# Self-attention with weighted values of float16 parts, queries and keys placed in three steps, and the work of all heads put in one repeating order

## The chip, the core and the metric

The program runs on one core of one Trainium2 chip. The metric is the device time of one execution, in microseconds (us). The core's engines run beside each other and wait for each other by semaphores only: TensorE (PE) multiplies, VectorE (DVE), ScalarE (ACT) and GpSimd (POOL) do the elementwise work, and SyncE (SP) starts DMA transfers. Each engine takes its instructions strictly in the order in which the program has them, so an instruction that waits holds up all that stand behind it.

## The reference

The kernel computes one layer over x of shape 8 x 512 x 256 in float32: self-attention, attention to a second input, and a block with eight experts. The change touches the first part alone:

```python
x = x + _L0_attn_ref(_layernorm(x, axis=-1), w_q, w_k, w_v, w_o)

q = jnp.einsum('ntc,hdc->nhtd', x, w_q)      # 16 heads of 64
k = jnp.einsum('ntc,hdc->nhtd', x, w_k)
v = jnp.einsum('ntc,hdc->nhtd', x, w_v)
a = jnp.einsum('nhtd,nhsd->nhts', q, k) / jnp.sqrt(dk)
a = jnp.where(mask, -jnp.inf, a)             # causal: keys after the query are masked
a = jax.nn.softmax(a, axis=-1)
y = jnp.einsum('nhts,nhsd->nthd', a, v)
return y.reshape(n, t, -1) @ w_o
```

## The kernel before

`self_attention` works in 32 units: 8 batches times 4 groups of 4 heads. A product of two float32 matrices is made of float16 parts (`split_terms`): each operand is a high part and the low part that rounding left over, and three matmuls (high-high, low-high, high-low) replace one. The steps of a unit are these, with the names that the rest of the text uses.

- Projections (`project_qk`, four calls; `project_v`, two). Each is 12 or 6 matmuls into a PSUM bank `pp`; ACT rounds the result to its high part (`a_nat_q`, `a_nat_k`), DVE writes the low part (`qk_low`, two instructions of 64 partitions each, straight to `QB` and `KA`). Values stay float32 in `V`.
- Placing. SP copies the high parts by eight DMAs of 128 KB to `QA`, `KA`, `KB` (`copy_qk`). A scores matmul then has the high and the low part of one side stacked on the 128 partitions.
- Maxima (`scores_for_max`, 16 per unit). A matmul of 128 queries by the keys up to them goes to a bank `pm`, and DVE takes the row maxima (`reduce_max`, an instruction and a short read of its accumulator). They are turned on PE, negated by ACT (`NMT`) and placed by two small DMAs in a row of `QB` (`place_max`), so that the scores come out of PE with the maximum taken off.
- Scores, exponentials, weighted values (`scores`, `exponentials`, `weighted_values`), 12 slots per unit, three per head: 128 keys by 512 queries, 128 by 384, and 128 by 256 with 128 by 128. Scores go to one of two banks `pS`, ACT writes the exponentials to one of four float32 buffers `PR`, and PE multiplies them with `V` in float32 into a bank `pa`. One half of each `V` tile is ones, so half of `pa` holds the row sums.
- Normalizing and the output projection: `reciprocals` (ACT: Ln, then Exp of its negative), `scale_values` (DVE), `split_values` (POOL), and once per batch `project_out`, 96 matmuls in one piece, and `residual`.

The order is written out by hand. Turn s of the loop holds the front of unit s (projections, placing, maxima) and the back of unit s-1 (scores to normalizing). Slot i of the turn issues the scores of slot i, then in slots 0, 1, 3 and 4 a projection, from slot 5 to 10 the 16 maxima, two or three at a time, and the weighted values of slot i-1. `project_out` of the previous batch stands whole in slot 6 of every fourth turn.

## Time and profile before

| | |
|---|---|
| time, median of 3 runs | 2320.03 us (2316.13 to 2321.22) |
| the profiled execution | 2315.4 us, its span 2313.7 us |
| PE busy over the span | 1958.2 us (85%) |
| DVE, ACT, POOL busy | 1397.7, 1194.2, 699.9 us |
| granted TensorE clock, mean | 0.934 of full speed |

The program has three parts, one after the other. Self-attention fills the first 1010 us. A row of the profile names the source line, the engine, the operation, what is written and what is read (`a_` are the tensors of self-attention), the shape, the count, busy time and the mean duration of one, and then how long the engine stood idle before such rows and for whom. Matmuls overlap: a row's duration is longer than the distance from one matmul's start to the next one's, and that distance is what a matmul costs in a full stream. In a timeline row the first number is the start, the second the duration, and the bracket at the end, where there is one, is the idle time before it with what ended it.

### The profile page before, as it was taken

To read this page: it belongs to the slowest core of one execution; us is meant where nothing else is said; L and a number is where in the kernel's file an instruction comes from. 1 tells how busy PE (TensorE), PEld (TensorE's weight loads), DVE (VectorE), ACT (ScalarE), POOL (GpSimd) and SP (SyncE) were. 2 spreads that over 40 slices of the span, in tenths; PEclk is the share of its full clock that TensorE was granted. 3 is DMA by queue.
4 is the path that set the end of the run, shared out by engine and by line. 5 is a ranking of instruction groups with operands and counts; after the bars stand their busy time and mean duration, and the time that the engine had idled before them with its cause. 6 is when DMAs were issued, how large, how long until landed. Compare 5 with 4: busy or idle time off the path is not lost. (4 is left out here: it accounts for less than half of the span.)

```text
span 2313.7 us, 37956 instructions
## 1 busy us (share of the span) xinstructions
PE 1958.2 (85%) x13464; PEld 1002.0 (43%) x13464; DVE 1397.7 (60%) x3126; ACT 1194.2 (52%) x2157; POOL 699.9 (30%) x693
## 2 busy tenths in 40 slices
PE   4899999999999999967999999847888887459973
PEld 2556565655565656542333233212333333236642
DVE  5665656564656565526878777735677876513344
ACT  2554545454545454534777777743555664125541
POOL 2111101110111111122333333124466666412266
PEclk8999999999999999987999899977999998779996
DMA  5111111111111021123223222200011201133355
GB/s 155 46 40 34 38 37 37 37 38 38 37 32 43 20 46 29 37 63 57 56 56 56 37 50 55 32 18 28 1 37 38 65 28 37 39 101 104 105 161 155
DMA packets 97082, 122.82 MB, mean 53 GB/s; under 512 B 14305, under 2 KB 73985, under 8 KB 96897
## 3 DMA queue, kind: packets, MB, share of 16 engines
q1 hardware_dynamic: 79872, 93.11, 17.1%
q0 software_dynamic: 6144, 16.79, 2.3%
q10 hardware_dynamic: 10880, 10.49, 1.4%
q8 instruction: 112, 1.84, 0.3%
q14 instruction: 74, 0.60, 0.1%
HBM read 52.64 MB, written 33.82 MB: 37 GB/s over the span
## 5 line engine op out<-in xcount | busy, mean ns | idle before, releaser
L1037 DVE TENSOR_REDUCE x_NM<-x_pm 128x1 f32<-128x512 f32 x512 | 342.6, 687 | 108.4 <-PE x_pm L780 106.3
L962 ACT ACTIVATE x_PR<-x_pS 128x512 f32<-128x512 f32 x512 | 300.9, 601 | 115.6 <-PE x_pS L796 108.9
L309 PE MATMUL a_pa<-a_PR,a_V 128*128 128x512 f32 (+3 forms) x1024 | 340.7, 440 | 0.7 <-ACT a_PR L389 0.3
L389 ACT ACTIVATE a_PR<-a_pS 128x384 f32<-128x384 f32 (+1 forms) x384 | 201.4, 525 | 206.7 <-PE a_pS L298 204.3
L471 DVE CUSTOM_DVE_ANT_0 a_pm<-a_pm,a_causal 128x128 f32<-128x128 f32 (+3 forms) x512 | 247.2, 509 | 84.9 <-PE a_pm L284 70.1
L544 POOL CAST a_YT_hi<-a_Y 128x512 f16<-128x512 f32 x64 | 40.2, 628 | 759.1 <-DVE a_Y L479 759.1
L780 PE MATMUL x_pm<-x_KT,x_QT 48*128 48x512 f16 x512 | 198.6, 406 | 22.7 <-DMA x_QT<-q_k_parts 22.0
L796 PE MATMUL x_pS<-x_QT,x_KT 49*128 49x512 f16 x512 | 194.2, 396 | 17.3 <-ACT x_PR L962 16.1
L479 DVE TENSOR_TENSOR a_Y<-a_pa,a_RS 64x512 f32<-64x512 f32 x128 | 88.0, 688 | 181.0 <-ACT a_RS L397 179.8
L309 PEld LDWEIGHTS a_pa<-a_PR,a_V 128*128 128x128 f32 x1024 | 174.7, 192 | 29.8 <-ACT a_PR L389 11.3
L284 PE MATMUL a_pm<-a_KA,a_QA 128*128 128x128 f16 (+3 forms) x512 | 142.5, 308 | 44.9 <-DVE a_NM L471 27.9
L808 PE MATMUL x_pa<-x_PR,x_V 128*32 128x256 f32 x2048 | 168.2, 401 | 1.7
L296 PE MATMUL a_pS<-a_QA,a_KA 128*128 128x512 f16 (+3 forms) x512 | 153.2, 299 | 1.7 <-DMA a_QB<-a_NMT 1.7
L395 ACT ACTIVATE a_RS<-a_pa 64x512 f32<-64x512 f32 x128 | 75.7, 592 | 144.1 <-PE a_pa L309 141.9
L297 PE MATMUL a_pS<-a_QB,a_KB 128*128 128x512 f16 (+3 forms) x512 | 146.5, 299 | 0.0
L796 PEld LDWEIGHTS x_pS<-x_QT,x_KT 49*128 49x128 f16 x512 | 46.7, 93 | 187.2 <-issue 89.4
L2279 PE MATMUL e_pH<-m_w_hi,e_xt 128*128 x320 | 109.7, 385 | 15.7 <-ACT e_xt L2327 6.6
L258 PE MATMUL a_pp<-a_xT_hi,a_wqk_hi 128*128 128x512 f16 x256 | 98.8, 386 | 23.2 <-DVE a_QB L461 15.8
L1774 ACT ACTIVATE f_PR<-f_pS 128x512 f32<-128x512 f32 x128 | 69.4, 594 | 83.3 <-PE f_pS L1624 83.3
L461 DVE SCALAR_TENSOR_TENSOR a_KA<-a_pp,a_nat_k 64x512 f16<-64x512 f32 x128 | 88.2, 689 | 36.1 <-ACT a_nat_k L377 35.2
L2369 DVE SCALAR_TENSOR_TENSOR e_TH<-e_TH,e_pH 128x512 f32<-128x512 f32 x40 | 27.5, 687 | 134.8 <-ACT e_TH L2333 134.8
L298 PE MATMUL a_pS<-mask_kq,idb 128*128 128x128 bf16 x512 | 105.5, 219 | 0.0
(360 smaller groups left out, 4519.4 us busy)
## 6 DMA issues: line engine op xcount, KB each, us to landing
a_QA<-a_nat_q SPq DMA_DIRECT2D x128, 128.0 KB, 2.3
e_xr<-sent SPq DMA_DIRECT2D x80, 128.0 KB
made<-e_eo ACTq DMA_DIRECT2D x40, 256.0 KB
a_KA<-a_nat_k SPq DMA_DIRECT2D x64, 128.0 KB, 2.3
a_KB<-a_nat_k SPq DMA_DIRECT2D x64, 128.0 KB, 2.4
x_KT<-q_k_parts SPq DMA_DIRECT2D x48, 128.0 KB, 4.3
x_QT<-q_k_parts SPq DMA_DIRECT2D x48, 128.0 KB, 4.4
f_w_stage<-in_w SPq DMA_DIRECT2D x12, 512.0 KB
```

The costliest lines, as they stand in the source:

```text
L284: eng.matmul(o, QA[:, par, side, pair, t * P:(t + 1) * P], KA[:, par, side, pair, 0:(t + 1) * P], start=True, stop=True).then_inc(s_mx, 1)
L296: eng.matmul(o, KA[:, par, side, pair, ks], QA[:, par, side, pair, qs], start=True, stop=False)
L297: eng.matmul(o, KB[:, par, side, pair, ks], QB[:, par, side, pair, qs], start=False, stop=False)
L309: m = eng.matmul(pa[j % 2][:, P * kc:T], V[:, u % 2, kc, j, :], PR[:, i % 4, at:at + T - P * kc], start=(kc == 0), stop=(kc == TT - 1))
L389: eng.activation(PR[:, i % 4, 0:n], pS[i % 2][:, 0:n], ACT.Exp, scale=SCALE).then_inc(s_e, 1)
L471: eng.tensor_tensor_reduce(out=pm[i % 2][:, 0:n], in0=pm[i % 2][:, 0:n], in1=causal[:, T - n:T], scale=1.0, scalar=NEG, op0=ALU.add, op1=A ...
L780: eng.matmul(ring_bank("max", v, n)[:, :], QT[r, par, pair, t * P:(t + 1) * P], KT[r, par, pair, :], start=True, stop=True).then_inc(s_mx, 1)
L796: eng.matmul(pS[i % 2][:, :], KT[r, par, pair, kc * P:(kc + 1) * P], QT[r, par, pair, :], start=True, stop=True).then_inc(s_s, 1)
L808: m = eng.matmul(pa[2 * D * j:2 * D * (j + 1), q], V[:, b % 2, kc, GH * g + j, :], PR[:, kc, j, q], start=(kc == 0 and half == 0), stop=(k ...
L962: eng.activation(PR[:, kc, j, :], pS[i % 2][:, :], ACT.Exp, scale=SCALE).then_inc(s_e, 1)
L1037: eng.tensor_reduce(NM[:, v % 2, c:c + 1], ring_bank("max", v, n)[:, :], AX.X, ALU.max, negate=True).then_inc(s_red, 1)
L2279: m = eng.matmul(pH[p % 2][:, h, :], xt[:, p % 2, h, x, kc, :], w13[ww][:, kc, bass.ds(e, 1), :].rearrange("p a f -> p (a f)"), start=(i = ...
```

## The change

The loop of turns is gone. Each engine has its steps as threads (for PE: weighted values, scores, maxima, projections), each step has a place in time from the table `PLACE`, repeated every `TURN`, and `side_by_side` merges the threads by these numbers. The numbers are sort keys only; nothing waits for a time. Beside the order, the steps themselves change:

- The exponential is computed twice from the same bank: once in float32 (`PR`, now three buffers) and once rounded to float16 (`P_hi`, four buffers). POOL subtracts them to the low part (`P_lo`). PE multiplies with three float16 matmuls per former float32 one. `V` has a high part from ACT and a low part from DVE. `LIFT` raises the exponentials by a constant factor that normalizing takes out again.
- A bank `pS` is free when the second exponential has read it (`s_eh`); weighted values wait for the low part (`s_el`).
- Low parts of queries and keys are written by one DVE instruction of 128 partitions to `nat[1]`, and DMAs place them as well: six for queries (`CQ`), four for keys (`CK`), two for the keys' second copy (`CKB`). `QA` and `QB` have three buffers.
- The output projection is cut to one tile of 128 rows per unit, 24 matmuls, five units later; `YT` has two buffers. The second half of the reciprocals is one instruction for two heads.
- The weights are staged in two buffers instead of four.

```diff
+def side_by_side(*threads):
+    at = [next(t, None) for t in threads]
+    while any(a is not None for a in at):
+        n = min((a, i) for i, a in enumerate(at) if a is not None)[1]
+        at[n] = next(threads[n], None)
...
-    weights = Weights(names, chunks, 4, 4 * C)
+    weights = Weights(names, chunks, 2, 4 * C)
...
-    QA, QB, KA, KB = (sb(n, [P, 2, 2, 2, T], F16) for n in ("QA", "QB", "KA", "KB"))
+    RQ = 3
+    QA, QB = (sb(n, [P, RQ, 2, 2, T], F16) for n in ("QA", "QB"))
+    KA, KB = (sb(n, [P, 2, 2, 2, T], F16) for n in ("KA", "KB"))
...
-    PR = sb("PR", [P, 4, T], F32)
+    RF, RH = 3, 4
+    PR = sb("PR", [P, RF, T], F32)
+    P16 = [sb(f"P_{n}", [P, RH, T], F16) for n in ("hi", "lo")]
...
+    TURN = 27.0
+    PLACE = {
+        ("PE", "QK"): (0, 0.988, 14.218, 17.436),
...
+        ("SP", "CK"): (21.044,),
...
+    }
...
+    def at(engine, step, u, i=0):
+        return u * TURN + PLACE[engine, step][i]
...
-            if i == 0:
-                eng.wait_ge(s_cp[par], CPS * (u // 2 + 1))
-                eng.wait_ge(s_lo, 4 * u + 4)
-                after(eng, s_ne, u)
...
-            after(eng, s_e, US * u + i - 1)
...
-        def weighted_values(u, i):
-            j, sl = i // NS, i % NS
-            eng.wait_ge(s_e, US * u + i + 1)
-            if sl == 0:
-                after(eng, s_y, GH * u + j - 1)
-            if i == 0:
-                eng.wait_ge(s_vout, 2 * u + 2)
-            for kc, at in SLOTS[sl]:
-                m = eng.matmul(pa[j % 2][:, P * kc:T], V[:, u % 2, kc, j, :], PR[:, i % 4, at:at + T - P * kc],
-                               start=(kc == 0), stop=(kc == TT - 1))
-            m.then_inc(s_av, 1)
+        def project_out(u):
+            b, t = (u - 5) // NG, (u - 5) % NG
+            for half in range(2):
+                yield at("PE", "WO", u, half)
+                if half == 0:
+                    if u == 5:
+                        eng.wait_ge(weights.split_done, NW)
+                    eng.wait_ge(s_yh, 2 * NG * (b + 1))
+                    eng.wait_ge(s_yl, 2 * NG * (b + 1))
+                    eng.wait_ge(s_vlo, min(2 * u + 1, 2 * NU))
+                    after(eng, s_xr, u - 5)
+                n = 12 * half
+                for pr in range(4 * half, 4 * half + 4):
+                    for w, y in split_terms(*(z[:, pr, :] for z in wo), *(z[:, b % 2, pr, t * P:(t + 1) * P] for z in YT)):
+                        m = eng.matmul(pp[0][:, 0:C], y, w, start=(n == 0), stop=(n == 23))
+                        n += 1
+            m.then_inc(s_wo, 1)
...
+                if i == 0:
+                    eng.wait_ge(s_cq[par], NCQ * (u // 2 + 1))
+                    eng.wait_ge(s_ck[par], NCK * (u // 2 + 1))
...
+                if i == 0:
+                    eng.wait_ge(s_ckb[par], NCKB * (u // 2 + 1))
+                    eng.wait_ge(s_nd[par], 32 * (u // 2 + 1))
+                after(eng, s_eh, US * u + i - 1)
...
+        def weighted_values(u):
+            for i in range(US):
+                yield at("PE", "AV", u, i)
+                j, sl = i // NS, i % NS
+                eng.wait_ge(s_el, US * u + i + 1)
+                if sl == 0:
+                    after(eng, s_y, GH * u + j - 1)
+                if i == 0:
+                    eng.wait_ge(s_vlo, 2 * u + 2)
+                for kc, a in SLOTS[sl]:
+                    for n, (v, p) in enumerate(((0, 0), (1, 0), (0, 1))):
+                        m = eng.matmul(pa[j % 2][:, P * kc:T], V[v][:, u % 2, kc, j, :], P16[p][:, i % RH, a:a + T - P * kc],
+                                       start=(kc == 0 and n == 0), stop=(kc == TT - 1 and n == 2))
+                m.then_inc(s_av, 1)
...
+        side_by_side(over(weighted_values), over(scores), over(scores_for_max), over(projections, NU + 5))
...
-        def exponentials(u, i):
-            n = slot_width(i % NS)
-            eng.wait_ge(s_s, US * u + i + 1)
-            after(eng, s_av, US * u + i - 3)
-            eng.activation(PR[:, i % 4, 0:n], pS[i % 2][:, 0:n], ACT.Exp, scale=SCALE).then_inc(s_e, 1)
+        def exponentials(u):
+            for i in range(US):
+                yield at("ACT", "E", u, i)
+                m, n = US * u + i, slot_width(i % NS)
+                eng.wait_ge(s_s, m + 1)
+                after(eng, s_el, m + 1 - RF)
+                eng.activation(PR[:, m % RF, 0:n], pS[i % 2][:, 0:n], ACT.Exp, scale=SCALE).then_inc(s_e, 1)
+                yield at("ACT", "H", u, i)
+                after(eng, s_av, m + 1 - RH)
+                eng.activation(P16[0][:, m % RH, 0:n], pS[i % 2][:, 0:n], ACT.Exp, scale=SCALE).then_inc(s_eh, 1)
...
-            for side in range(2):
-                rows = slice(side * D, (side + 1) * D)
-                dst, at = (QB, side) if qk == 0 else (KA, 1 - side)
-                i = eng.scalar_tensor_tensor(out=dst[at * D:(at + 1) * D, u % 2, side, pair, :], in0=pp[c % 2][rows, :],
-                                             scalar=1 / WS, in1=nat[qk][rows, pair, :], op0=ALU.mult, op1=ALU.subtract)
...
+                eng.scalar_tensor_tensor(out=nat[1][qk][:, pair, :], in0=pp[c % 2][:, :], scalar=1 / WS,
+                                         in1=nat[0][qk][:, pair, :], op0=ALU.mult, op1=ALU.subtract).then_inc(s_lo, 1)
...
+        def exp_low(u):
+            for i in range(US):
+                yield at("POOL", "LO", u, i)
+                m, n = US * u + i, slot_width(i % NS)
+                eng.wait_ge(s_e, m + 1)
+                eng.wait_ge(s_eh, m + 1)
+                after(eng, s_av, m + 1 - RH)
+                eng.tensor_tensor(P16[1][:, m % RH, 0:n], PR[:, m % RF, 0:n], P16[0][:, m % RH, 0:n],
+                                  ALU.subtract).then_inc(s_el, 1)
...
+        def copies(u):
             par = u % 2
+            yield at("SP", "CQ", u)
+            if u == 0:
+                eng.wait_ge(s_pre, NPRE)
+            eng.wait_ge(s_hi, 4 * u + 2)
+            eng.wait_ge(s_lo, 4 * u + 2)
+            after(eng, s_s, US * (u - RQ + 1))
+            for side, own in enumerate(sides):
+                for rows in sides:
+                    eng.dma_start(QA[rows, u % RQ, side, :, :], nat[0][0][own, :, :]).then_inc(s_cq[par], 16)
+                eng.dma_start(QB[own, u % RQ, side, :, :], nat[1][0][own, :, :]).then_inc(s_cq[par], 16)
+            yield at("SP", "CK", u)
             eng.wait_ge(s_hi, 4 * u + 4)
+            eng.wait_ge(s_lo, 4 * u + 4)
             after(eng, s_s, US * (u - 1))
+            for side, own in enumerate(sides):
+                eng.dma_start(KA[own, par, side, :, :], nat[0][1][own, :, :]).then_inc(s_ck[par], 16)
+                eng.dma_start(KA[sides[1 - side], par, side, :, :], nat[1][1][own, :, :]).then_inc(s_ck[par], 16)
+            yield at("SP", "CKB", u)
+            for side, own in enumerate(sides):
+                eng.dma_start(KB[own, par, side, :, :], nat[0][1][own, :, :]).then_inc(s_ckb[par], 16)
+            yield at("SP", "NP", u)
             eng.wait_ge(s_ne, u + 1)
...
```

How the engines' orders stand, first PE in the middle of a turn. L296 and L448 are scores, L284 and L429 maxima, L309 and L464 weighted values. Before:

```order
L309 MATMUL a_pa<-a_PR,a_V 128x256 [waits a_exp]
L309 MATMUL a_pa<-a_PR,a_V 128x128
L296 MATMUL a_pS<-a_QA,a_KA 128x384 [waits a_exp]
L297 MATMUL a_pS<-a_QB,a_KB 128x384
L298 MATMUL a_pS<-mask_kq,idb 128x128
L284 MATMUL a_pm<-a_KA,a_QA 128x384 [waits a_red]
L284 MATMUL a_pm<-a_KA,a_QA 128x512 [waits a_red]
L309 MATMUL a_pa<-a_PR,a_V 128x512 [waits a_y,a_exp]
```

After:

```order
L429 MATMUL a_pm<-a_KA,a_QA 128x128 [waits a_red]
L464 MATMUL a_pa<-a_P_hi,a_V_hi 128x512 [waits a_y,a_exp_lo]
L464 MATMUL a_pa<-a_P_hi,a_V_lo 128x512
L464 MATMUL a_pa<-a_P_lo,a_V_hi 128x512
L448 MATMUL a_pS<-a_QA,a_KA 128x384 [waits a_exp_hi]
L449 MATMUL a_pS<-a_QB,a_KB 128x384
L450 MATMUL a_pS<-mask_kq,idb 128x128
L429 MATMUL a_pm<-a_KA,a_QA 128x256 [waits a_red]
L429 MATMUL a_pm<-a_KA,a_QA 128x384 [waits a_red]
L464 MATMUL a_pa<-a_P_hi,a_V_hi 128x384 [waits a_exp_lo]
L464 MATMUL a_pa<-a_P_hi,a_V_lo 128x384
L464 MATMUL a_pa<-a_P_lo,a_V_hi 128x384
```

A weighted-values matmul has become three, and it waits for the low part of the exponentials from POOL instead of the exponentials from ACT. The weighted values stand some slots behind their scores, where they stood one slot behind.

ACT in a turn: L389, L509 and L512 are exponentials, L395/L397 and L522/L525 the reciprocals, L377 and L489 high parts, L421 the maxima's copy. Before:

```order
L389 ACTIVATE a_PR<-a_pS 128x384 [waits a_av,a_scores] x2
L389 ACTIVATE a_PR<-a_pS 128x512 [waits a_av,a_scores]
L395 ACTIVATE a_RS<-a_pa 64x512 [waits a_y,a_av]
L397 ACTIVATE a_RS<-a_RS 64x512 [waits a_ln]
L389 ACTIVATE a_PR<-a_pS 128x384 [waits a_av,a_scores] x2
L421 ACTIVATE a_NMT<-a_pm 16x128 [waits a_nm_placed1,a_nm_turned]
L395 ACTIVATE a_RS<-a_pa 64x512 [waits a_y,a_av]
L397 ACTIVATE a_RS<-a_RS 64x512 [waits a_ln]
```

After:

```order
L509 ACTIVATE a_PR<-a_pS 128x384 [waits a_exp_lo,a_scores]
L489 ACTIVATE a_nat_q_hi<-a_pp 128x512 [waits a_q_placed0,a_qk]
L512 ACTIVATE a_P_hi<-a_pS 128x384 [waits a_av]
L489 ACTIVATE a_nat_q_hi<-a_pp 128x512 [waits a_qk]
L509 ACTIVATE a_PR<-a_pS 128x384 [waits a_exp_lo,a_scores]
L512 ACTIVATE a_P_hi<-a_pS 128x384 [waits a_av]
L522 ACTIVATE a_RS<-a_pa 64x512 [waits a_y,a_av]
L509 ACTIVATE a_PR<-a_pS 128x512 [waits a_exp_lo,a_scores]
L512 ACTIVATE a_P_hi<-a_pS 128x512 [waits a_av]
L509 ACTIVATE a_PR<-a_pS 128x384 [waits a_exp_lo,a_scores]
L512 ACTIVATE a_P_hi<-a_pS 128x384 [waits a_av]
L522 ACTIVATE a_RS<-a_pa 64x512 [waits a_y,a_av]
```

Each slot now has two exponentials, the second waiting for a free `P_hi` buffer, and the high parts of the next unit's queries stand between them.

PE where the maxima of a unit begin; the first of them waits for the placed queries and keys. Before:

```order
L296 MATMUL a_pS<-a_QA,a_KA 128x128
L297 MATMUL a_pS<-a_QB,a_KB 128x128
L298 MATMUL a_pS<-mask_kq,idb 128x128
L284 MATMUL a_pm<-a_KA,a_QA 128x128 [waits a_nm_out,a_red,a_lo,a_copied0]
L284 MATMUL a_pm<-a_KA,a_QA 128x256 [waits a_red]
L309 MATMUL a_pa<-a_PR,a_V 128x384 [waits a_exp]
L284 MATMUL a_pm<-a_KA,a_QA 128x384 [waits a_red]
L296 MATMUL a_pS<-a_QA,a_KA 128x512 [waits a_exp]
L297 MATMUL a_pS<-a_QB,a_KB 128x512
L298 MATMUL a_pS<-mask_kq,idb 128x128
```

After:

```order
L448 MATMUL a_pS<-a_QA,a_KA 128x256 [waits a_exp_hi]
L449 MATMUL a_pS<-a_QB,a_KB 128x256
L450 MATMUL a_pS<-mask_kq,idb 128x128
L448 MATMUL a_pS<-a_QA,a_KA 128x128
L449 MATMUL a_pS<-a_QB,a_KB 128x128
L450 MATMUL a_pS<-mask_kq,idb 128x128
L429 MATMUL a_pm<-a_KA,a_QA 128x128 [waits a_nm_out,a_red,a_k_placed1,a_q_placed1]
L429 MATMUL a_pm<-a_KA,a_QA 128x256 [waits a_red]
L448 MATMUL a_pS<-a_QA,a_KA 128x512 [waits a_exp_hi]
L449 MATMUL a_pS<-a_QB,a_KB 128x512
L450 MATMUL a_pS<-mask_kq,idb 128x128
L429 MATMUL a_pm<-a_KA,a_QA 128x384 [waits a_red]
```

The maxima began in slot 5 and came in a dense run. Now two maxima stand between the scores of slots 2 and 3 of the unit before, and the rest is spread over the turn that follows.

## Rows read from the trace of the kernel before

**Rows 1.** The page: busy time of each engine, share of the span, instructions

```profile
PE 1958.2 (85%) x13464; PEld 1002.0 (43%) x13464; DVE 1397.7 (60%) x3126; ACT 1194.2 (52%) x2157; POOL 699.9 (30%) x693
```

**Rows 2.** One stretch: length, busy us (count) of each engine, clock, DMA share, GB/s

```profile
48.90:974.30 925.40, 867.69 (x5276) 533.97 (x5274) 552.87 (x1487) 463.47 (x848) 130.82 (x136) 1.00 0.16 37
```

**Rows 3.** Timeline of ACT: the copies of the maxima of units 0 and 31

```profile
48.70 0.27 ACT L421 ACTIVATE a_NMT<-a_pm 16x128 f16<-16x128 f32 x1 [13.49 <-PE a_pm L356]
...
974.10 0.25 ACT L421 ACTIVATE a_NMT<-a_pm 16x128 f16<-16x128 f32 x1
```

**Rows 4.** Waits from 62 to 960 us: engine, line, for whom, total us, times, longest

```profile
PE a_pm L284 <- DVE a_NM L471: 23.2, 67, 1.5
...
PE a_pp L258 <- DVE a_QB L461: 15.0, 30, 0.5
...
PE a_pm L284 <- DMA a_KB<-a_nat_k: 9.4, 10, 1.7
```

**Rows 5.** Timeline of PE between 529.9 and 551 us

```profile
529.94 0.38 PE L258 MATMUL a_pp<-a_xT_lo,a_wqk_hi 128*128 128x512 f16 x1
530.16 1.02 PE L309 MATMUL a_pa<-a_PR,a_V 128*128 128x512 f32 x2
531.01 0.27 PE L296 MATMUL a_pS<-a_QA,a_KA 128*128 128x256 f16 x1
...
531.23 0.22 PE L298 MATMUL a_pS<-mask_kq,idb 128*128 128x128 bf16 x1
531.29 0.22 PE L296 MATMUL a_pS<-a_QA,a_KA 128*128 128x128 f16 x1
...
533.95 0.82 PE L309 MATMUL a_pa<-a_PR,a_V 128*128 128x256 f32 x4
534.61 0.33 PE L296 MATMUL a_pS<-a_QA,a_KA 128*128 128x384 f16 x1
...
539.19 0.81 PE L309 MATMUL a_pa<-a_PR,a_V 128*128 128x384 f32 x2
539.84 0.33 PE L284 MATMUL a_pm<-a_KA,a_QA 128*128 128x384 f16 x1
...
540.49 0.27 PE L323 MATMUL a_pp<-a_wo_hi,a_YT_hi 128*128 128x256 f16 x1
...
550.97 0.43 PE L284 MATMUL a_pm<-a_KA,a_QA 128*128 128x512 f16 x2
```

**Rows 6.** Groups of ACT by shape: count, busy us, mean ns

```profile
L389 ACT ACTIVATE a_PR<-a_pS 128x384 f32<-128x384 f32 x256 | 125.3, 490 | 88.1 <-PE a_pS L298 85.8
...
L377 ACT ACTIVATE a_nat_q<-a_pp 128x512 f16<-128x512 f32 x64 | 38.2, 597 | 39.8 <-PE a_pp L258 38.4
```

**Rows 7.** Groups of DVE and POOL; the last from the page, all shapes

```profile
L461 DVE SCALAR_TENSOR_TENSOR a_QB<-a_pp,a_nat_q 64x512 f16<-64x512 f32 x128 | 88.2, 689 | 17.0 <-ACT a_nat_q L377 14.3
...
L546 POOL TENSOR_TENSOR a_YT_lo<-a_Y,a_YT_hi 128x512 f16<-128x512 f32 x64 | 74.0, 1156 | 5.1
...
L471 DVE CUSTOM_DVE_ANT_0 a_pm<-a_pm,a_causal 128x128 f32<-128x128 f32 (+3 forms) x512 | 247.2, 509 | 84.9 <-PE a_pm L284 70.1
```

**Rows 8.** Timeline of SP, two copies; and the page's issues, last number landing

```profile
570.18 0.60 SPq L585 DMA_DIRECT2D a_QA<-a_nat_q  x1
570.82 0.59 SPq L586 DMA_DIRECT2D a_KA<-a_nat_k  x1
...
a_KB<-a_nat_k SPq DMA_DIRECT2D x64, 128.0 KB, 2.4
```

**Rows 9.** Timeline of PE: start of the last output projection

```profile
997.02 0.28 PE L323 MATMUL a_pp<-a_wo_hi,a_YT_hi 128*128 128x256 f16 x1 [3.98 <-POOL a_YT_lo L546]
...
998.21 0.42 PE L323 MATMUL a_pp<-a_wo_hi,a_YT_hi 128*128 128x256 f16 x1
```

**Rows 10.** Timeline of DVE and POOL in the first 14 us

```profile
11.69 2.22 DVE L121 SCALAR_TENSOR_TENSOR a_wqk_lo<-a_w_stage,a_wqk_hi 128x1024 f16<-128x1024 f32 x1 [2.15 <-ACT a_wqk_hi L115]
...
10.70 2.13 POOL L538 TENSOR_TENSOR a_xn_lo<-a_xn,a_xn_hi 128x1024 f16<-128x1024 f32 x1 [2.59 <-ACT a_xn_hi L370]
```

More of the change, by code:

```diff
@@ L245, in project_qk, with over, transpose_x @@
+    def over(thread, n=NU):
+        for i in range(n):
+            yield from thread(i)
+    def tensor_program(eng):
+        def transpose_x(b, half):
+            eng.wait_ge((s_xhi, s_xlo)[half], b + 1)
+            if half == 0:
+                after(eng, s_vlo, 2 * NG * b)
+            else:
+                after(eng, s_xr, NG * b - 5)
+            turned(eng, pp[1 - half], xn16[half], k).then_inc(s_xt, 1)
         def project_qk(u, c):
             b, g = u // NG, u % NG
+            if u < NG and c == 0:
+                eng.wait_ge(weights.split_done, 2 * u + 1)
@@ new lines, in projections @@
+        def projections(u):
+            b, g = u // NG, u % NG
+            if g == 0 and u < NU:
+                for h in range(2):
+                    yield at_turned("PE", b, h)
+                    transpose_x(b, h)
+            for c in range(4 if u < NU else 0):
+                yield at("PE", "QK", u, c)
+                project_qk(u, c)
+            for h in range(2 if u < NU else 0):
+                yield at("PE", "V", u, h)
+                project_v(u, h)
+            if u >= 5:
+                yield from project_out(u)
@@ L429, in vector_program, with split_weights @@
+        def split_weights():
+            for n in range(NW):
+                yield at_split(n)
+                weights.high(eng, n)
+        eng.preload_act_table_set("natural_log_exp_and_others")
+        side_by_side(over(reciprocals), over(exponentials), over(maxima_out), over(projections), over(x_high, B), split_weights())
     def vector_program(eng):
         def statistics(b):
+            if b < 2:
+                eng.wait_ge(s_x[b], 16)
             for t in range(TT):
@@ new lines, in reduce_max @@
+        def reduce_max(u):
+            for i in range(4 * GH):
+                yield at("DVE", "MX", u, i)
+                eng.wait_ge(s_mx, 16 * u + i + 1)
+                if i == 0:
+                    eng.wait_ge(s_causal, 1)
+                    after(eng, s_nt, u)
+                n = (i % TT + 1) * P
+                eng.tensor_tensor_reduce(out=pm[i % 2][:, 0:n], in0=pm[i % 2][:, 0:n], in1=causal[:, T - n:T], scale=1.0,
+                                         scalar=NEG, op0=ALU.add, op1=ALU.max, accum_out=NM[:, column(i)]).then_inc(s_red, 1)
@@ new lines, in scale_values, with split_weights @@
+        def scale_values(u):
+            for j in range(GH):
+                pair, q = j // 2, 2 * u + j // 2
+                yield at("DVE", "Y", u, j)
+                eng.wait_ge(s_rc, q + 1)
+                after(eng, s_yl, q - 1)
+                outs, _ = rows_of(j)
+                eng.tensor_tensor(Y[outs, pair, :], pa[j % 2][outs, :], RS[outs, pair, :], ALU.mult).then_inc(s_y, 1)
+        def split_weights():
+            for n in range(NW):
+                yield at_split(n) + 1.3
+                weights.low(eng, n)
@@ L599, in sync_program @@
         eng.dma_start(x_res[:, TT:B * TT, :], x_dram[:, TT:B * TT, :]).then_inc(s_x[1], 16)
-        weights.load(eng, 4)
-        weights.load(eng, 5)
-        for s in range(NU):
-            copy_qk(s)
-            if s < 2:
-                for n in SPLIT_AT[s].values():
-                    weights.load(eng, n + weights.buffers)
-            place_max(s)
+        side_by_side(over(copies), load_weights())
     with nc.Block() as block:
```

529 lines of the change are left out of this document (223 added, 306 removed).

## The prediction

> **What bounds the kernel now.** I read the page first. PE is busy 85% of the span, DVE 60%, ACT 52% [rows 1]. Self-attention alone is denser: between the copy of unit 0's maxima and that of unit 31's [rows 3], PE is busy 867.7 of 925.4 us (94%), DVE 552.9 (60%), ACT 463.5 (50%), POOL 130.8 (14%), with the clock granted in full [rows 2]. The other three engines have room, PE has none. These 925.4 us are 31 turns, so 29.85 us a turn.
>
> A matmul's duration overlaps the next one, so PE's real load comes from distances between starts [rows 5]. Float16: 512 columns 0.22 us (529.94 to 530.16), 128 columns 0.06 (531.23 to 531.29), and 256 columns 0.109, since 96 of them fill the 10.48 us from 540.49 to 550.97. By columns I take 0.216, 0.163, 0.109 and 0.056 for 512, 384, 256 and 128. Float32: 512 columns 0.85 (530.16 to 531.01), 384 columns 0.65 (539.19 to 539.84), 256 and 128 together 0.66 (533.95 to 534.61). Per unit, from these:
> queries and keys, 24 of 512: 5.2;
> values, 24 of 256: 2.6;
> output projection, a quarter of those 10.48 us: 2.6;
> scores, per head 2 x 0.544 + 4 x 0.056 = 1.31: 5.2;
> maxima, 4 x 0.544: 2.2;
> transposes: 0.3;
> weighted values in float32, 4 x 2.16: 8.6.
> That is 26.8 us of PE work in a turn of 29.85; 3.0 us a turn are stalls. Where they are, the table of waits says: the maxima wait for DVE to empty a bank (23.2 us in 67 waits), the projections for DVE's low parts (15.0 us, 30 waits), and the first maximum for the placed keys (9.4 us, 10 waits) [rows 4]. The table holds only what is left after the tails of matmuls are taken off, so it shows less than 3.0 a turn.
>
> **Part 1: weighted values of three float16 matmuls.** Per head 3 x 0.544 = 1.63 instead of 2.16 us, per unit 6.5 instead of 8.6: 2.1 us less in each turn. All of it is on PE, which is the bound, so it counts in full: 32 x 2.1 = 68 us. PE's work becomes 24.7 us a turn. A matmul of 128 columns needs a new weight tile each time; in this trace 128-column matmuls with a new tile each start 0.06 apart, 531.23 to 531.29 [rows 5], so I add nothing for weight loads. The Trainium skill says otherwise (TensorE: Matmul & The Clock Gate, Back-to-back issue gap): in a stream of weight load and matmul pairs, 128 columns come to about 81 ns each, 512 to about 131. By its 81 ns the 12 new matmuls of 128 columns less the 4 that they replace would add about 0.3 us a turn, some 10 us in all; the trace disagrees, both at 128 and at 512 columns.
>
> **Part 2: what makes the parts.** ACT gets 12 more exponentials per unit. The rounded output costs what a float16 copy out of PSUM costs, 597 ns at 512 [rows 6], and 490 at 384: 4 x 0.60 + 8 x 0.49 = 6.3 us; two reciprocals fewer give back 1.2, at the 0.6 us of a 512-wide instruction. ACT's load was 463.5/31 = 15.0, it becomes 20.1. POOL gets 12 subtractions: 1.16 us at 512 [rows 7]; between that and 2.13 for 1024 [rows 10] the slope is 1.9 ns an element, so 0.91 at 384: 11.9 us, on top of 130.8/31 = 4.2: 16.1. DVE: low parts of queries and keys, four of 128 partitions instead of eight of 64, at 689 ns each [rows 7] (partitions cost nothing, it seems: 1.35 ns a column there with 64, and 509 ns for 320 columns on average with 128): -2.8; low parts of values, four of 256 elements, at most 0.69 and at least half of it, I take 0.42: +1.7. DVE stays at 17.8 - 1.1 = 16.7. All fit under 24.7; none becomes the bound by its sum.
>
> A place where sums would lie is a port held by two engines. DVE's low part of the first weights took 2.22 us while POOL's subtraction of 2.13 us ran [rows 10]; 689 ns for 512 elements would make about 1.4 for its 1024, so it was held up. The Trainium skill (SBUF — State Buffer, Who interferes with whom) has the rule: a DVE instruction with two inputs in SBUF contends with a POOL instruction that reads SBUF, one with at most one does not. By that rule, the trace agrees: POOL's 12 subtractions meet DVE instructions that all take one operand from PSUM, and only the ten weight splits of the first turns can collide, about 0.8 us each, hidden for most.
>
> **Part 3: the stalls that stay.** This is the term with the widest bounds: from 0.5 us a turn (nearly all covered, each engine having room) to the 3.0 of before. I walked one turn in the new order, PE's place being the sum of the costs above from the first query projection on, and others starting 0.2 us after PE's last column (a handover ACT to DVE or POOL to PE under 0.1). Three places are tight:
> - Scores of slot 10. PE is there after 10.1 us. The bank is free when slot 8's second exponential is done; its scores end at 7.8, but a logarithm stands ahead (weighted values 5 end at 7.35, so 7.6 to 8.2), then the first exponential to 8.7, the shared reciprocal to 9.3, the second exponential to 9.8. Stall 0 to 0.2.
> - The first maximum, place 19.8, behind the key copies. The last key projection ends at 13.6; ACT, then DVE give its low part at 15.3; SP places the maxima of the unit before, is free at 16.0, and issues four copies, 0.64 us apart (570.18 to 570.82). The last is issued at 17.9 and lands 2.4 us later [rows 8]: 20.3. Stall 0.5.
> - Scores of slot 3, place 19.9, want the second exponential of slot 1, done at 20.2, since a copy of values stands between. Stall 0.4, partly the same time as the one before.
> Once per batch DVE does the statistics and the normalizing (eight instructions of 256 columns, at least half of the 689 ns each, so some 3 us and over in two pieces), with maxima queued behind it and PE behind them, and the transposes wait for the residual: some 2.5 us, 0.6 a turn. With 0.2 for handovers elsewhere this is 1.6 us a turn. Before, 16 maxima stood in six slots and DVE (247.2/32 = 7.7 us of work for them [rows 7], the reads of the accumulator not counted) was too slow there; now they lie over 22 of 27 units of the plan, so the largest of the old waits goes, and the output projection no longer stands in one piece. Turn: 24.7 + 1.6 = 26.3 us. Against 29.85 that is 3.55 less, times 31: -110 us.
>
> **Part 4: the two ends.** Up to the copy of unit 0's maxima (48.7 us [rows 3]) little changes: POOL's presets are longer and ahead of the layer norm, DVE has half the low-part instructions, the weight splits lie earlier. I take 0, bounds -4 and +4. From unit 31's copy (974.1 [rows 3]) to the stage's end at 1010 are 36 us. Its middle becomes bound by ACT: per head 2 x 1.58 + 0.6 + 0.3 = 4.1, four heads 16.3, as long as the stretch before. POOL's step adds 1.2 us, two scalings after one shared reciprocal 0.7, and the four tiles now use one bank in turn, each waiting for its residual: 3 x 0.75 = 2.3. PE idles before these matmuls, as it did for 3.98 us, after which the clock fell to half (the same matmul took 0.28 us, then 0.42) [rows 9]. Sum: +4, bounds 0 and +10.
>
> **Sum.** 2315.4 - 110 + 4 = 2209 us for the profiled execution. It lies 0.2% under the median of the runs (2320.0), so 2214 for the median. Attention to the second input and the experts are left as they are.
>
> **Rivals.**
> - The feeders bind. Exponentials are handed over twice per slot, banks are released later, and every queue is strict; the walk misses such knots. Then stalls stay at 3.0 and only the work goes: 31 x 2.1 = 65 less, 4 more: 2254, or 2259 by the median. For: ACT at 20.1 and DVE at 16.7 of 26 are close to what they feed. Against: the loads leave each at least 6 us of room a turn. 17%.
> - The floor is reached. Stalls of 0.5: 25.2 a turn, -144 + 4: 2175, or 2180. For: places with slack are the rule in the walk. Against: the key copies' 0.5 alone. 9%.
> - The clock. If waits gather to several us in one place of a turn, PE drops to 1.2 GHz for a while, as at 998.2 [rows 9], where 256 columns took 0.42 instead of 0.28 us. If that lasts for 16 such matmuls, each 0.107 later, it is 1.7 us a turn, 2209 + 53 = 2262, or 2267. For: the stage's end shows it. Against: full clock over 925 us with more stalls than I expect [rows 2]. 3%.
> - Slower. One mechanism: weighted values of a slot wait for the low part from POOL. From the scores' start to it: 0.44 + 0.2 + 0.53 + 0.53 + 0.07 + 0.99 = 2.8 us, against 1.2 before. If the rows between them don't cover it, PE waits 12 times a turn. 24.7 + 12w passes 29.85 at w = 0.43 us; with w = 0.55, half of the added 1.6 less some cover, the turn is 31.3: 2315 + 45 + 4 = 2364, or 2369. Against: two to five other steps stand between scores and their weighted values. 4%.
> - That the early query copies do nothing, since the first maximum waits for the keys anyway, is so in my walk, and in the sum.
>
> **How the numbers follow.** The forecast, a turn between 25.4 and 27.3, has 67%, and by itself 2186 to 2245. Range for 8 in 10: from a turn of 25.1 (2177) to the rival of the feeders with the later bounds of the ends (2268). A measurement tells about 0.2% from no change here, 5 us. Faster 94%, the same 2%, slower 4%.
>
> **What would show it.** Right: distances of 0.22 and 0.06 us within the three float16 matmuls; copies of the maxima 26.3 us apart; POOL near 60% busy and ACT near 77% between them; self-attention ends at about 904 us; no group of DVE or POOL longer than given above. Wrong: PE waiting for `P_lo` in many slots, scores waiting for `P_hi`, turns of 28 us or more, or a granted clock under 0.95 in the middle of the stage.

## The result, and the profile after

| | median of runs | ratio to before, 95% interval |
|---|---|---|
| before | 2320.62 us (2316.13 to 2331.82) | |
| after | 2390.03 us (2385.92 to 2392.54) | 1.0293 [1.0267, 1.032] |

The change made the kernel 2.9% slower; I had forecast 4.6% faster and given slower 4%. The profiled execution took 2385.9 us.

First the copies of the maxima on ACT, which answer to [rows 3]: a group's shortest, median and longest ns, and the first and the last start.

```profile
L501 ACT ACTIVATE a_NMT<-a_pm x32: 250/250/267, 53.4 to 1049.5; 16x128 f16<-16x128 f32 x32
```

That is 996.1 us for 31 turns, 32.13 us each; before it was 29.85, the forecast 26.3. The stage's last residual is at 1089.7 instead of 1010.1, 79.6 us later: 70.7 of it are turns, 4.7 the start (53.4 for 48.7), 4.2 the end (40.2 us after unit 31's copy, before 36.0). The rest of the program, in which nothing was changed, is 9 us shorter (1303.6 and 1294.5 us) with the same number of instructions. That goes with TensorE's clock: in the ten profiles of this document the rest takes 1293 to 1300 us where its granted clock is 0.90 (after is one of them) and 1304 to 1310 us where it is 0.89 (before is one). Why it is now the one and now the other stays open.

Between these copies, in the columns of [rows 2] (length; busy us and count of PE, its weight loads, DVE, ACT and POOL; clock, DMA share, GB/s):

```profile
53.40:1049.50 996.10, 832.46 (x5714) 530.40 (x5714) 518.79 (x1497) 564.16 (x1152) 490.06 (x505) 0.92 0.23 52
```

Per turn DVE is busy 16.7 us and POOL 15.8, as forecast (16.7, 16.1); ACT 18.2, with 20.1 forecast: its neighbouring instructions overlap in the records, whose durations add up to 636 us where ACT is busy for 564, and 636 us are 20.5 a turn. So no engine became the bound by its load. PE is busy for 84% of the stretch and had 94%. And its granted clock is 0.92 on average: of its two levels, 2.4 and 1.2 GHz, it had the lower one for some 160 us ((1 - 0.92) x 2 x 996).

The waits of PE in the stage's middle, 24 turns, in the columns of [rows 4]. The projections' wait for DVE's low parts of queries, 15.0 us there, is gone:

```profile
PE a_pm L429 <- issue: 105.7, 24, 5.6
PE a_pm L429 <- DVE a_NM L605: 15.7, 7, 2.6
PE a_pp L83 <- DVE a_V_lo L591: 1.4, 1, 1.4
PE a_pp L83 <- DVE x_res L567: 0.8, 5, 0.2
```

One wait a turn, of 4.4 us on average, and it has no name: `issue` means that the profile shows nothing that PE waited for. By its line, and one per unit, it is the first maximum. In `scores_for_max` that is the matmul with `wait_ge(s_cq...)` and `wait_ge(s_ck...)`, so it waits for the transfers of queries and keys. The timeline of PE at one of them (start, duration, line, [idle before]):

```profile
511.05 0.22 PE L450 MATMUL a_pS<-mask_kq,idb 128*128 128x128 bf16 x1
515.75 0.48 PE L429 MATMUL a_pm<-a_KA,a_QA 128*128 128x128 f16 x2 [4.48 <-issue]
516.02 0.63 PE L448 MATMUL a_pS<-a_QA,a_KA 128*128 128x512 f16 x1
516.45 0.63 PE L449 MATMUL a_pS<-a_QB,a_KB 128*128 128x512 f16 x1
```

Behind the wait the two matmuls of 512 columns start 0.43 us apart, twice the 0.22 of [rows 5]: PE runs at 1.2 GHz. What SP did meanwhile:

```profile
505.91 1.41 SPq L703 DMA_DIRECT2D a_QB<-a_NMT  x2
507.43 1.17 SPq L687 DMA_DIRECT2D a_QA<-a_nat_q_hi  x2
508.63 0.81 SPq L688 DMA_DIRECT2D a_QB<-a_nat_q_lo  x1
509.49 1.24 SPq L687 DMA_DIRECT2D a_QA<-a_nat_q_hi  x2
510.76 0.60 SPq L688 DMA_DIRECT2D a_QB<-a_nat_q_lo  x1
511.48 0.53 SPq L694 DMA_DIRECT2D a_KA<-a_nat_k_hi  x1
512.05 0.60 SPq L695 DMA_DIRECT2D a_KA<-a_nat_k_lo  x1
512.68 0.60 SPq L694 DMA_DIRECT2D a_KA<-a_nat_k_hi  x1
513.32 0.60 SPq L695 DMA_DIRECT2D a_KA<-a_nat_k_lo  x1
```

The six copies of queries stand directly before the four of keys, and all ten behind the placing of the last unit's maxima (L703). The last key copy is issued at 513.32, and 2.4 us later, at 515.7, PE goes on: the landing time of [rows 8]. And SP's own waits, for the whole stretch:

```profile
SPq L703 <- ACT a_NMT L501: 672.5, 31, 26.9
```

SP stood 672.5 of 996 us before the placing, 21.7 us a turn, with the query copies queued behind it. Their data had long been there: the low part of the next unit's queries is ready at 530.95, and its first copy is issued at 540.74, behind the placing at 539.22. The reason is in `copies(u)`: it is one thread, and its steps CQ, CK, CKB and NP of a unit come one after the other. `side_by_side` merges threads by their numbers, but it can't take CQ of unit u+1 (14.36 + 27 = 41.36) ahead of NP of unit u (45.93) when both are steps of the same thread.

### The profile page after: what moved, and what is told of

Its sections match the earlier page's. It is cut to its first block and busy times, and to the rows that moved or that the text cites. A ratio compares the mean times of both kernels' runs of the same rounds, so it can differ in the third digit from the quotient of the medians.

```text
span 2384.2 us, 40460 instructions
## 1 busy us (share of the span) xinstructions
PE 1920.8 (81%) x13976; PEld 1000.1 (42%) x13976; DVE 1368.5 (57%) x3150; ACT 1301.4 (55%) x2477; POOL 1074.4 (45%) x1077
## 5 line engine op out<-in xcount | busy, mean ns | idle before, releaser
L646 POOL TENSOR_TENSOR a_P_lo<-a_PR,a_P_hi 128x384 f16<-128x384 f32 (+1 forms) x384 | 378.2, 998 | 443.1 <-ACT a_P_hi L512 342.9
L509 ACT ACTIVATE a_PR<-a_pS 128x384 f32<-128x384 f32 (+1 forms) x384 | 204.3, 532 | 301.1 <-PE a_pS L450 295.6
L429 PE MATMUL a_pm<-a_KA,a_QA 128*128 128x128 f16 (+3 forms) x512 | 151.8, 328 | 167.6 <-issue 139.5
L888 PE MATMUL x_pm<-x_KT,x_QT 48*128 48x512 f16 x512 | 197.2, 404 | 20.7 <-DMA x_QT<-q_k_parts 20.1
L512 ACT ACTIVATE a_P_hi<-a_pS 128x384 f16<-128x384 f32 (+1 forms) x384 | 203.9, 531 | 8.2 <-PE a_pa L464 4.9
L448 PE MATMUL a_pS<-a_QA,a_KA 128*128 128x512 f16 (+3 forms) x512 | 161.5, 316 | 4.9 <-ACT a_P_hi L512 3.0
L449 PE MATMUL a_pS<-a_QB,a_KB 128*128 128x512 f16 (+3 forms) x512 | 156.6, 318 | 0.0
L464 PE MATMUL a_pa<-a_P_hi,a_V_lo 128*128 128x512 f16 (+3 forms) x512 | 155.1, 303 | 0.0
L464 PE MATMUL a_pa<-a_P_hi,a_V_hi 128*128 128x512 f16 (+3 forms) x512 | 153.6, 303 | 0.3 <-POOL a_P_lo L646 0.2
L464 PE MATMUL a_pa<-a_P_lo,a_V_hi 128*128 128x512 f16 (+3 forms) x512 | 148.3, 303 | 0.0
L429 PEld LDWEIGHTS a_pm<-a_KA,a_QA 128*128 128x128 f16 x512 | 49.3, 103 | 217.8 <-issue 150.7
L1214 POOL TENSOR_TENSOR x_res<-x_res,x_OT 128x256 f32<-128x256 f32 x32 | 23.2, 726 | 231.7 <-DVE x_OT L1154 231.7
L2445 POOL TENSOR_TENSOR e_H_lo<-e_TH,e_H_hi 128x512 f16<-128x512 f32 x40 | 46.3, 1158 | 155.9 <-ACT e_H_hi L2379 155.8
```

Source lines behind the costliest of these rows:

```text
L429: eng.matmul(pm[i % 2][:, 0:(t + 1) * P], QA[:, u % RQ, side, pair, t * P:(t + 1) * P], KA[:, par, side, pair, 0:(t + 1) * P], start=True, ...
L464: m = eng.matmul(pa[j % 2][:, P * kc:T], V[v][:, u % 2, kc, j, :], P16[p][:, i % RH, a:a + T - P * kc], start=(kc == 0 and n == 0), stop=( ...
L509: eng.activation(PR[:, m % RF, 0:n], pS[i % 2][:, 0:n], ACT.Exp, scale=SCALE).then_inc(s_e, 1)
L512: eng.activation(P16[0][:, m % RH, 0:n], pS[i % 2][:, 0:n], ACT.Exp, scale=SCALE).then_inc(s_eh, 1)
L646: eng.tensor_tensor(P16[1][:, m % RH, 0:n], PR[:, m % RF, 0:n], P16[0][:, m % RH, 0:n], ALU.subtract).then_inc(s_el, 1)
L888: eng.matmul(ring_bank("max", v, n)[:, :], QT[r, par, pair, t * P:(t + 1) * P], KT[r, par, pair, :], start=True, stop=True).then_inc(s_mx, 1)
```

## Experiments

Theory, Q in the expectations: SP's strict queue, with six copies ahead of the keys in one thread, costs nearly all of the 4.4 us, and the wait brings the lower clock, which costs some 2.6 us more. Rivals: the wait is PE's own, which gets its instructions late there (F); the feeders bind as soon as this wait goes (B); the clock falls by something else, the wait being only where it shows; the low parts on POOL; the float16 matmuls and their weight tiles. The runs below were made at other times than after; the medians of before taken beside them are 2317.7 us (e1 to e4) and 2319.2 us (e5 to e8), beside after 2320.6, so times from different groups compare to some 3 us.

### e1: the placing of the maxima is a thread of its own

```diff
                 eng.dma_start(KB[own, par, side, :, :], nat[0][1][own, :, :]).then_inc(s_ckb[par], 16)
+
+        def place_max(u):
+            par = u % 2
             yield at("SP", "NP", u)
...
-        side_by_side(over(copies), load_weights())
+        side_by_side(over(copies), over(place_max), load_weights())
```

> Placing the maxima is taken out of the copies' thread on SP, so that SP's queue follows the table: queries of unit u+1, then the maxima of unit u, then the keys of unit u+1. Theory Q (SP's strict queue makes the first maximum wait): the wait of about 4.6 us in every turn before the first maximum falls to under 1 us, the granted clock goes back from 0.91 to about 1.00 in the stage, a turn takes 25.3 to 26.5 us instead of 32.1, and the whole 2384 - 31 x 6.1 = 2195 us (2180 to 2215). Rival F (PE fails to get its instructions there; the profile names no releaser): the wait stays, 2384. Rival B (the feeders would bind anyway as soon as this wait goes): the wait goes, but waits for P_hi, P_lo or DVE take its place, a turn of 28 us or more, 2260 or more.

2207.99 us (2203.79 to 2212.14), 0.9552 [0.9504, 0.96]. SP's timeline, in which the queries of the next unit (519.20) now stand ahead of the placing (530.54):

```profile
502.30 1.41 SPq L706 DMA_DIRECT2D a_QB<-a_NMT  x2
503.81 0.53 SPq L694 DMA_DIRECT2D a_KA<-a_nat_k_hi  x1
504.38 0.60 SPq L695 DMA_DIRECT2D a_KA<-a_nat_k_lo  x1
505.02 0.60 SPq L694 DMA_DIRECT2D a_KA<-a_nat_k_hi  x1
505.66 0.60 SPq L695 DMA_DIRECT2D a_KA<-a_nat_k_lo  x1
...
519.20 1.10 SPq L687 DMA_DIRECT2D a_QA<-a_nat_q_hi  x2
...
530.54 1.41 SPq L706 DMA_DIRECT2D a_QB<-a_NMT  x2
532.06 0.53 SPq L694 DMA_DIRECT2D a_KA<-a_nat_k_hi  x1
```

PE at the first maximum, PE's waits over 28 turns, and the stretch between the copies of the maxima, each as above:

```profile
508.09 0.33 PE L429 MATMUL a_pm<-a_KA,a_QA 128*128 128x128 f16 x2 [0.43 <-issue]
508.25 0.38 PE L448 MATMUL a_pS<-a_QA,a_KA 128*128 128x512 f16 x1
508.47 0.38 PE L449 MATMUL a_pS<-a_QB,a_KB 128*128 128x512 f16 x1
```

```profile
PE a_pm L429 <- DVE a_NM L605: 15.7, 7, 2.6
PE a_pm L429 <- issue: 14.1, 28, 1.2
```

```profile
53.40:865.00 811.60, 767.76 (x5714) 500.37 (x5715) 518.62 (x1497) 563.96 (x1153) 488.70 (x505) 0.99 0.27 63
```

The same work on each engine as after, to 2 us on DVE, ACT and POOL, in 811.6 instead of 996.1 us. The wait is 14.1 / 28 = 0.5 us, the clock 0.99, the turn 26.18. That one thread holds 182 us (2390.0 - 2208.0; the two spans differ by the same), and the low parts and the float16 matmuls are cleared of the slowdown, since both stand unchanged. F and B fall with them: PE's instructions are the same, and no other wait took the place of this one.

### e2: the wait stays, but PE is kept busy in it

```diff
                 if i == 0:
+                    after(eng, s_ne, u)
+                    for _ in range(16):
+                        eng.matmul(pm[0][:, 0:P], k.id32[:, :], k.id32[:, :], start=True, stop=True)
                     eng.wait_ge(s_cq[par], NCQ * (u // 2 + 1))
                     eng.wait_ge(s_ck[par], NCK * (u // 2 + 1))
-                    after(eng, s_ne, u)
```

The 16 matmuls a unit write to a bank that the next maximum overwrites; only the time they take matters. In float32 each shows as two rows.

> The changed kernel with 16 float32 matmuls of 128 columns (0.22 us each, 3.5 us) ahead of the wait for the placed queries and keys, into a bank that is overwritten next. They do no useful work. Theory Q with the clock as a second cost: the wait of 4.6 us is only filled, not longer; PE stays busy, the granted clock goes from 0.91 to about 1.00, and the 31 turns lose the half-speed share, about 2.7 us each: 2384 - 85 = 2300 us (2285 to 2325). If the clock costs nothing beside the wait: 2384 (2375 to 2390). Rival F (PE held up by its own instruction supply): 16 more matmuls come on top, 2384 + 110 = 2490.

2346.09 us (2334.15 to 2349.27), 1.0127 [1.007, 1.0184], so 44 us less than after, with more work on PE, but above the 2285 to 2325 expected.

```profile
54.50:996.60 942.10, 880.61 (x6706) 613.56 (x6707) 518.70 (x1497) 564.17 (x1153) 490.17 (x505) 0.99 0.24 55
```

PE's rows of the fillers (columns of the page's groups) and of the wait:

```profile
L427 PE MATMUL a_pm<-id 128*128 128x128 f32 x992 | 117.5, 277 | 0.0
```

```profile
PE a_pm L431 <- issue: 28.6, 26, 1.8
```

The clock is back at 0.99, so PE's idleness in the wait is what lowered it, not the order or the load of the other engines. The turn fell by 1.7 us to 30.39 (942.1 / 31), less than the 2.6 that the clock had cost (80 us in 31 turns): the fillers take 117.5 / 31 = 3.8 us a turn and a wait of 28.6 / 26 = 1.1 us is left, together 0.5 longer than the wait of after. The other 0.4 us a turn isn't explained.

### e3: two of the six copies behind the keys

```diff
-    NCQ, NCK, NCKB = 6 * 16, 4 * 16, 2 * 16
+    NCQ, NCK, NCKB = 4 * 16, 4 * 16, 4 * 16
...
-                eng.dma_start(QB[own, u % RQ, side, :, :], nat[1][0][own, :, :]).then_inc(s_cq[par], 16)
...
                 eng.dma_start(KB[own, par, side, :, :], nat[0][1][own, :, :]).then_inc(s_ckb[par], 16)
+                eng.dma_start(QB[own, u % RQ, side, :, :], nat[1][0][own, :, :]).then_inc(s_ckb[par], 16)
```

DVE's next low part waits for the later copy instead (`s_ckb`).

> The changed kernel with the two copies of the queries' low parts (QB, which the maxima do not read) moved behind the keys' copies; the place of the maxima in the queue is unchanged. Theory Q, by dose: the last key copy is issued 2 x 0.64 = 1.3 us earlier, the wait falls from 4.6 to 3.3 us, so 40 us less, and up to 40 more if the shorter wait leaves the clock up: 2345 (2300 to 2350). Rival F: 2384. Rival B: under 40 us, since other waits fill in: 2365 or more.

2337.37 us (median of 10, 2321.27 to 2352.13), 1.009 [1.0055, 1.0124], within the range expected. The profile is of the shortest of the ten, with a mean clock of 0.919 over the whole program where the others had 0.903 to 0.918, so it shows e3 at its best.

```profile
PE a_pm L429 <- issue: 84.5, 28, 3.9
```

```profile
52.20:986.10 933.90, 812.70 (x5714) 520.49 (x5715) 518.49 (x1497) 564.21 (x1153) 489.55 (x505) 0.94 0.24 55
```

The wait went from 4.4 to 84.5 / 28 = 3.0 us, by 1.4; two issues are 1.3. The clock rose only to 0.94, (1 - 0.94) x 2 x 934 = 112 us at the lower level: 3 us of waiting once a turn still brings it down, and over the whole program the clock of seven of the other nine runs was lower still, 0.903 to 0.914.

### e4: a fourth float16 pass, on e1

```diff
-                    for n, (v, p) in enumerate(((0, 0), (1, 0), (0, 1))):
+                    for n, (v, p) in enumerate(((0, 0), (1, 0), (0, 1), (1, 1))):
...
-                                       start=(kc == 0 and n == 0), stop=(kc == TT - 1 and n == 2))
+                                       start=(kc == 0 and n == 0), stop=(kc == TT - 1 and n == 3))
```

> As e1_own_thread, with a fourth float16 matmul per weighted-values tile (low part by low part), 0.544 us per head, 2.18 us a turn more PE work; it adds a term that the other kernels leave out. Against e1_own_thread: if PE is the bound in the turn, +2.18 x 32 = 70 us (60 to 75); if the feeders are (rival B), under 35 us. It is also about the PE work that float32 weighted values would have, so it prices the float16 parts: the gain that three passes have over them.

2255.05 us, 0.974 [0.969, 0.9791]: 47 us over e1, between what was expected if PE is the bound (60 to 75) and if it isn't (under 35). The pass is 2.2 us of PE work a turn (4 heads x 0.544), 68 us in 31 turns; the turn grew by 1.66 to 27.84. A quarter of it fell into waits that were there: the wait before the first maximum, 14.1 us in 28 turns of e1, is 4.0 us in as many here.

### e5 and e8: ACT issues the placing

```diff
             eng.activation(NMT[:, :], pm[0][0:16, 0:P], ACT.Copy, scale=-1.0, bias=LIFT).then_inc(s_ne, 1)
+            eng.wait_ge(s_ne, u + 1)
+            for side in range(2):
+                r = D if side == 0 else 0
+                eng.dma_start(QB[r:r + 1, u % RQ, side, :, :].rearrange("o a t -> o (a t)"),
+                              NMT[8 * side:8 * side + 8, :]).then_inc(s_nd[u % 2], 16)
...
-            yield at("SP", "NP", u)
-            eng.wait_ge(s_ne, u + 1)
...
```

e5 is this edit on the changed kernel; the placing goes from SP's thread.

> The changed kernel with the two DMAs that place the maxima issued by ACT right behind its copy of the maxima, so that SP's queue has only the copies of queries and keys. Theory Q: the queue order is mended in another way than in e1_own_thread, so the 4.6 us wait goes too; the keys' copies no longer stand behind the maxima either, so the rest of the wait (0.6 us a turn in e1_own_thread) goes as well: 2190 to 2205 us, up to 18 less than e1_own_thread's 2208. Against it: ACT's queue is held for the two issues, some 1.3 us a turn; if ACT is near the bound, 2210 to 2250.

2213.58 us, 0.9543 [0.9505, 0.9582], no better than e1's 2207.99; what was expected of theory Q alone, 2190 to 2205, missed, and the counter-argument's 2210 to 2250 holds it. So taking the placing out of the copies' way by another edit brings back nearly as much, 176 us against the 182 of e1. The wait before the first maximum no longer shows among PE's, but one at the scores does:

```profile
PE a_pm L429 <- DVE a_NM L610: 15.7, 7, 2.6
PE a_pS L448 <- issue: 10.8, 28, 0.7
PE a_pS L448 <- ACT a_P_hi L517: 2.7, 7, 0.8
```

The 28 waits for `issue` are one a turn, at the first scores of a unit, which have waits for transfers too (`s_ckb`, `s_nd`). Issued on ACT and then awaited by PE:

```profile
512.79 1.29 ACTq L505 DMA_DIRECT2D a_QB<-a_NMT  x2
515.90 0.38 PE L448 MATMUL a_pS<-a_QA,a_KA 128*128 128x512 f16 x1 [0.38 <-issue]
```

The second of the two placings is issued at about 513.4, half of the 1.29 us later, and PE goes on 2.5 us after it. So the scores wait for the placed maxima to land, not for exponentials; the rows for `a_P_hi` are 7 waits and 2.7 us. One landing is exchanged for another: 10.8 + 2.7 us here, 14.1 in e1. e8 is e5 with e7's edit.

> e5_maxima_by_act and e7_norm_spread together, a candidate for the fastest. If both act where they are expected, on different waits, they add: 2180 to 2195. If they overlap or ACT's queue takes it back: 2195 to 2210.

2203.31 us, 0.9498 [0.9461, 0.9536], in the range expected if ACT's queue takes it back, and some 10 us over e7 alone (2193.58).

### e6: the new order, weighted values in float32, on e1

```diff
-    V = [sb(f"V_{n}", [P, 2, TT, GH, P], F16) for n in ("hi", "lo")]
+    V = [sb("V", [P, 2, TT, GH, P], F32)]
...
-                    for n, (v, p) in enumerate(((0, 0), (1, 0), (0, 1))):
-                        m = eng.matmul(pa[j % 2][:, P * kc:T], V[v][:, u % 2, kc, j, :], P16[p][:, i % RH, a:a + T - P * kc],
-                                       start=(kc == 0 and n == 0), stop=(kc == TT - 1 and n == 2))
+                    m = eng.matmul(pa[j % 2][:, P * kc:T], V[0][:, u % 2, kc, j, :], PR[:, i % RF, a:a + T - P * kc],
+                                   start=(kc == 0), stop=(kc == TT - 1))
...
-        side_by_side(over(split_values), over(exp_low), over(norm, B))
+        side_by_side(over(split_values), over(norm, B))
```

The second exponential and the low parts of the values go with it, and there are four `PR` buffers.

> As e1_own_thread, but with the weighted values in float32 as before the change: no second exponential, no P_lo, no V_lo, one float32 matmul per tile, in the new order and with the copies in three steps. It splits the change. PE work of a turn 26.8 us. If PE's work is all that the float16 parts change, about e4_four_passes: 2255 (2245 to 2275), so the order and the placing give about 60 us and the float16 parts about 47. If the float16 parts' handovers cost much, this kernel comes close to e1_own_thread's 2208 (2215 to 2235). Beside it, a port theory: with no P_lo on POOL, the normalizing on DVE takes 408 ns an instruction again; in the four kernels with P_lo it took 750 to 1240 whenever POOL ran beside it. If the length came from something else in the new order, it stays over 700.

2240.88 us, 0.9657 [0.9619, 0.9695], between the two ranges expected; the turn is 27.42 us, from 55.2 to 905.2. So order and placing alone bring 78 us against before, and the float16 parts 33 more (e1).

### e7: the normalizing spread out, on e1

```diff
-            yield at_first("XN", b)
-            eng.wait_ge(s_rstd, b + 1)
-            after(eng, s_xlo, b)
             for t in range(TT):
+                yield at_first("XN", b) + (1.3 * t - 1.5 if b else 0)
+                if t == 0:
+                    eng.wait_ge(s_rstd, b + 1)
+                    after(eng, s_xlo, b)
```

> As e1_own_thread, with the four normalizing instructions of a batch on DVE at four places 1.3 apart instead of one behind the other. In e1_own_thread they hold DVE for 3.3 us once per batch, and PE then waits 2.6 us for a maximum. If that block is the cause of the 2.6 us: 7 batches x about 2 = 14 us less, 2195 (2190 to 2203). If the wait only moves: 2208.

2193.58 us (2190.38 to 2194.51), 0.9459 [0.9422, 0.9496]: 14 us under e1 and the fastest version here, faster than both kernels. Maxima are no longer queued behind all four:

```profile
PE a_pm L429 <- issue: 14.0, 28, 1.2
PE a_pm L429 <- DVE a_NM L606: 8.9, 7, 1.4
```

The wait for `a_NM`, 15.7 us in seven batches in e1, is 8.9. The stretch between the copies of the maxima is 13.2 us shorter than in e1 (798.4 us), and this wait is 6.8 of them. Some 3 more are the clock. Two of e1's seven waits of 2.6 us were followed by half speed, with a clock of 0.57 from 420 to 424 us and of 0.62 from 632 to 636; in e7, where these waits are at most 1.4 us, the clock is 1.00. The first of the two in e1:

```profile
420.70 0.61 PE L429 MATMUL a_pm<-a_KA,a_QA 128*128 128x512 f16 x1 [2.58 <-DVE a_NM L605]
421.10 0.42 PE L448 MATMUL a_pS<-a_QA,a_KA 128*128 128x256 f16 x1
```

The 3 us are (1 - 0.57) x 4 + (1 - 0.62) x 4; the remaining 3 aren't explained.

## Why the prediction was wrong

The step that failed is the second tight place of the walk in part 3: "The first maximum ... SP places the maxima of the unit before, is free at 16.0, and issues four copies ... Stall 0.5." It issues ten. The walk gave the wait 0.5 us; it was 4.4, and with it came a lower clock that the sum had at nothing. I took the query copies as gone already, by the numbers of the table, and did not ask which steps can be merged at all; in the order of SP's instructions, six copies stood between. Measured, at 515.75: placing done and queries begun at 507.43, keys begun at 511.48, so 4.05 us later; 4.05 + 0.43 is the wait of 4.48. The last sentence of the rivals, that the early query copies do nothing, is this cause with the wrong price: they were not early, and so not free.

What follows from it, per turn: 24.7 of PE's work, 4.4 of this wait instead of 0.5, and 80 / 31 = 2.6 for the lower clock are 31.7; 32.13 was measured. With e3: 24.7 + 3.0 + 56 / 31 = 29.5, measured 30.13. The rest in both, 0.4 to 0.6 us, is less than the 1.1 that the walk had for its other stalls; that some of those fall into the long wait is likely, but no run shows it.

The other steps, read on e1, where only this one is put right:

- Turn 26.18, forecast 26.3; time 2208, forecast 2214. The first maximum waits 0.5 us, forecast 0.5; the wait for `a_NM` once a batch is 15.7 / 7 = 2.2 us, forecast some 2.5.
- But the sum of -110 us for the turns hid two errors that cancel. The part from float16 was 65 us; between e6 and e1 it is 31 x (27.42 - 26.18) = 38. The part from stalls was 44; from before to e6 it is 31 x (29.85 - 27.42) = 75. Stalls in the float32 version of the new order are 27.42 - 26.8 = 0.6 us a turn, in the float16 one 1.5: the parts bring back stalls, and the weighted values are not worth their PE work in full. Two of these stalls have names: the wait for `a_NM` is 15.7 us in e1 and 3.3 in e6, the one before the first maximum 14.1 and 6.1, together 0.7 of the 0.9 us a turn. e4 says the same from the other side, 47 of 68 us. That the turn of e1 came within 0.1 us of the forecast is luck.
- Low parts on POOL: 916 ns at 384 and 1163 at 512, forecast 0.91 and 1.16. Low parts of values on DVE: 418 ns, forecast 0.42.

```profile
L646 POOL TENSOR_TENSOR a_P_lo<-a_PR,a_P_hi 128x384 f16<-128x384 f32 x248 | 225.7, 916 | 270.0 <-ACT a_P_hi L512 267.7
L646 POOL TENSOR_TENSOR a_P_lo<-a_PR,a_P_hi 128x512 f16<-128x512 f32 x124 | 144.2, 1163 | 171.8 <-ACT a_PR L509 96.5 <-ACT a_P_hi L512 73.8
L591 DVE SCALAR_TENSOR_TENSOR a_V_lo<-a_pp,a_V_hi 128x256 f16<-128x256 f32 x124 | 46.7, 418 | 1.8 <-ACT a_V_hi L494 0.9
```

- The end, +4 with bounds 0 and +10: +4.2. The start, 0 with bounds -4 and +4: +4.7, just outside.
- By the 81 ns at 128 columns that the prediction sets against its own, eight more such matmuls at 25 ns each would be 0.2 us a turn and 6 us in all, not 0.3 and 10. It was in no sum.
- The rival of the clock named the right mechanism ("if waits gather to several us in one place of a turn") with 1.7 us a turn; it was 2.6. It was given 3% because the walk showed no place where waits gather. The rival named slower, PE waiting for `P_lo`, did not come: no such wait is among PE's.
- "POOL's 12 subtractions meet DVE instructions that all take one operand from PSUM" is wrong for the normalizing (below).

## What to carry to other kernels

Where threads are merged by keys, write out one queue's real order for a full period before costing a wait: a step can't pass an earlier step of its own thread, whatever its key, and a transfer that waits for a late result holds up every one behind it. Where PE waits for `issue` once per unit at a matmul that waits for transfers, look at the issuing queue: count the copies between its last wait and the one needed, add one landing, and add the price of the lower clock from rows. And read a forecast's terms apart: a sum can be right to 0.3% with both of its terms off by 30 us.
